# Graph network on one core: in the steps of passes 1 to 4, the gathered group ahead of the stored blocks on TensorE

## The reference

```python
edge_index = jnp.stack([src, dst])
x = _layernorm(x + _L0_gnn_ref(x, src, dst, edge_weight, ...), axis=-1)   # weighted sum over edges, two matrices
x = _layernorm(x + _L1_gnn_ref(x, edge_index, ...), axis=-1)              # three layers: sum, W1, relu, W2, layer norm
x = _layernorm(x + _L2_gnn_ref(x, ..., src, dst), axis=-1)                # sum with degrees, then top-2 of 64 experts, batch norm
x = _layernorm(x + _L3_gnn_ref(x, src, dst, edge_weight, ...), axis=-1)   # weighted sum over edges, one matrix
return x
```

## Time and profile before

| | |
|---|---|
| median of 3 runs | 5157.87 us |
| lowest, highest | 5154.81, 5174.32 us |
| span of the profiled execution | 5775.2 us |
| its own time | none given beside the span |
| TensorE, busy | 4680.6 us, 81% |
| VectorE, busy | 3836.1 us, 66% |
| GpSimd, busy | 3422.4 us, 59% |
| ScalarE, busy | 2434.9 us, 42% |

### The profile page before, as it was taken

How to read it: one execution, slowest core, us unless ns; L and a number is a source line. 1 busy time by engine, 2 the same in 40 slices (tenths; PEclk the granted TensorE clock), 3 DMA queues, 4 the chain that set the end, 5 groups by cost and what they waited for, 6 DMA issues and landing times. The chain is left out here.

```text
span 5775.2 us, 83539 instructions
## 1 busy us (share of the span) xinstructions
PE 4680.6 (81%) x25279; PEld 3860.8 (67%) x25279; DVE 3836.1 (66%) x12440; ACT 2434.9 (42%) x6047; POOL 3422.4 (59%) x3425
## 2 busy tenths in 40 slices
PE   4988986678888788877888788885799867999897
PEld 3777864478777566655666567664799735777775
DVE  6788888457777587746888635456789655444453
ACT  3888875333332233323444333331455413333332
POOL 5566666656665555666666566664345454666665
PEclk8999988889998899988999889997899968999998
DMA  5333333487778767787878877774668533333333
GB/s 149 109 113 118 113 121 118 149 254 222 222 225 282 216 201 208 213 273 244 247 242 243 296 240 220 224 219 144 223 214 264 165 81 104 98 98 98 96 98 88
DMA packets 545371, 1047.08 MB, mean 181 GB/s; under 512 B 105274, under 2 KB 308792, under 8 KB 544636
## 3 DMA queue, kind: packets, MB, share of 16 engines
q0 software_dynamic: 221664, 684.44, 40.7%
q1 hardware_dynamic: 305978, 341.48, 18.0%
q10 hardware_dynamic: 17280, 15.74, 0.8%
HBM read 927.95 MB, written 114.65 MB: 181 GB/s over the span
## 5 line engine op out<-in xcount | busy, mean ns | idle before, releaser
L2412 POOL DMA_INDIRECT slot_rows<-planes,REC x1800 | 1743.1, 968 | 1017.9 <-issue 476.5
L2964 ACT ACTIVATE wide_blocks<-HH 128x512 fp32r<-128x512 uint8 x1344 | 739.6, 573 | 1046.8 <-PE PS L2516 429.3
L2516 PE MATMUL PS<-plane_rows,wide_blocks 128*128 128x512 f32 x3528 | 1027.0, 432 | 172.2 <-ACT wide_blocks L2964 124.0
L2516 PEld LDWEIGHTS PS<-plane_rows,wide_blocks 128*128 128x128 f32 x3528 | 687.5, 203 | 368.0 <-ACT wide_blocks L2964 152.7
L2412 POOL DMA_INDIRECT ring<-in_x,REC x555 | 536.7, 967 | 313.0 <-issue 142.9
L2412 POOL DMA_INDIRECT ring<-table,REC x486 | 466.2, 959 | 320.2 <-issue 212.6
L2494 PE MATMUL PS<-ring,pick 128*128 128x256 f32 x2082 | 561.7, 405 | 64.3 <-DMA ring<-table,REC 25.5
L2581 PE MATMUL PS<-HH 128*128 128x256 f32 x2058 | 506.2, 388 | 7.8 <-issue 5.5
L2494 PEld LDWEIGHTS PS<-ring,pick 128*128 128x128 f32 x2082 | 404.6, 203 | 155.6 <-issue 51.7
L3122 DVE TENSOR_SCALAR slot_picks<-iotab,REC 128x128 fp32r<-128x128 bf16 x1800 | 413.1, 302 | 137.5 <-remote 71.1
L2929 ACT ACTIVATE HH<-iota,HH 128x128 bf16<-128x128 f32 (+1 forms) x962 | 329.2, 391 | 338.1 <-remote 176.4
(11 more groups left out here) (380 smaller groups left out, 8980.8 us busy)
## 6 DMA issues: line engine op xcount, KB each, us to landing
HH<-dense_blocks SPq DMA_DIRECT2D x672, 112.0 KB
HH<-in_L_gnn_w SPq DMA_DIRECT2D x128, 512.0 KB
plane_rows<-planes SPq DMA_DIRECT2D x64, 768.0 KB
planes<-HN SPq DMA_DIRECT2D x188, 256.0 KB
slot_rows<-planes,REC POOLq DMA_INDIRECT x1800
dense_blocks<-HH SPq DMA_DIRECT2D x24, 784.0 KB
expert_outputs<-ring ACTq DMA_DIRECT2D x120, 128.0 KB
ring<-in_x,REC POOLq DMA_INDIRECT x555
```

Source lines behind the costliest of these rows:

```text
L2412: pool.indirect_dma_start(to, None, planes[k] if dense else tables[k], bass.IndirectOffsetOnAxis(ap=at_rows, axis=0)).then_inc(s_slot[slot ...
L2516: last = mm(bank(5 + n % 2, RP), WIDE[:, at_block:at_block + P], plane(0, t, RP), start=t == 0, stop=t == NT - 1)
L2964: fn(WIDE[:, e % XA * XW:e % XA * XW + w], AB[n % QA][:, lo:lo + w], ACT.Copy).then_inc(s_ax, 1)
```

## The change

In each step of `one_pass` on TensorE, the call of `products` moves from behind the two calls of `dense` to ahead of them. In passes 0 and 5 there are no stored blocks in steps that have gathered groups, and the blocks of the extra steps at a pass's end have no group beside them, so these keep their order. No other engine's program changes.

```diff
             def one_pass(k):
                 for g in range(STEPS[k]):
+                    if g < GROUPS[k]:
+                        products(k, g)
                     if k in DENSE_PASSES:
                         dense(k, blocks(g))
                     if k < 4 and g >= GROUPS[k]:
                         dense(k + 1, head_blocks(g - GROUPS[k]))
-                    if g < GROUPS[k]:
-                        products(k, g)
                     if g == 1:
                         pe.wait_ge(s_w, w_count(k))
```

## The result

The changed kernel takes 5179.72 us (median) against 5158.84 us for the kernel before on the same chip: ratio 1.0035, 95% interval [1.0024, 1.0045]. That is 21 us slower by the medians and 18 us by the ratio, within the half per cent that was called no change, and 17.7 us above the forecast. One of its six executions took 15779 us; ratio and interval leave it out, and without it the median would be 5179.33 us.

The account below looks back on a forecast made before the run. TensorE was taken as busiest, idling before stored blocks. Terms 7.7 - 5.8 + 3 - 3 + 3 = +4.9 us of span, times 0.893 = +4.4, gave 5162 us; range 5118 to 5202.

Parts of the forecast that it names:

- What bounds the kernel now: TensorE busiest, 4680.6 of 5775.2 us; in the middles it idles before stored blocks, never before gathered groups.
- The order as a ring: Only the gathered group moves among stored blocks (D) and remaining work (E) on TensorE; whole-turn waits keep their length.
- Stored blocks waiting for ScalarE, -3 us: Middles: stored blocks sometimes gain 0.70 us where ScalarE was held by a copy or relu; ends nothing and 112 us.
- The start, +7.7 us: Four pass starts: step 0's stored blocks move behind the first gather's wait, 1.92 us each warm; 13.6 us in all cold.
- The tail, -5.8 us: Tails of passes 1 to 3: step 137's stored blocks, 1.92 us each, are hidden behind gathers; pass 4 gains nothing.
- SyncE and the DMA queues, +3 us: Pass ends: SyncE's plane reloads start 2.6 us later, taken as 1 us at each of three boundaries; worst 7.8.
- E nearer to D, +3 us: Layer and hidden groups follow stored blocks 0.70 us sooner and may wait for ScalarE, mainly pass 3; ends 0 and 206.
- VectorE's operand for a gathered tile, 0: Before the transposes: gathered group lies 1.92 us further ahead, but VectorE is busy, so no gain; ends -34.7 and 0.
- (a): Middles, faster: gathered groups fill waits before stored blocks, 80 to 112 us of span, about 5078 us; chance 0.14.
- (b): Middles, slower: layer and hidden groups wait for ScalarE, 0.70 us each, 59 us in all, 5211 us; chance 0.12.
- (c): Pass ends, slower: cold start, no tail gain, late reloads, 23 us, 5179 us; chance 0.06 beyond the bound.
- (d): TensorE, slower: a late gather holds stored blocks; 0.0 us in pass 4's trace, counted inside the forecast, no separate chance.

Follow-up runs that it names:

- the second profile: The kernel before, unchanged, run and profiled once more: 5159.29 us, ratio 0.9996.
- four pairs: Old against changed order: as they were, ScalarE's roots before widenings, four widened-piece places, both; changed order costs +0.35%, +0.25%, +0.19%, +0.14%.
- both edits: ScalarE's roots ahead of widenings plus four widened-piece places for three, against the kernel before: old order 5151.59 us (0.9978), changed order 5157.74 us (0.9992).

## Why the prediction was right or wrong

**The number held, the sum did not.** 5179.72 us lies in the range of 5118 to 5202 and inside the band of no change, which had 0.68. But the forecast was 5162, and none of its terms is where the 21 us came from: it was the width of the band that held, and not the sum.

**"What bounds the kernel now": half right.** TensorE is the busiest engine, but the idle time "before the stored blocks" came from a stretched execution. In an undisturbed one, idle before L2516 and L2519 is 14.8 and 7.2 us in all, and what TensorE waits for in the middles is VectorE: 36.3 us before the histogram (L2598 for L3310) in pass 2, 53.8 us before the transposes (L2619 for L3391) in pass 3. After the change these are 39.2 and 60.1 us. Nor is it so that "a gathered group never keeps anything waiting in the middle": in pass 1 of the second profile the gathered rows are what TensorE waits for most, 24.3 us. The 617 us were seen, and answered with a factor of 0.893 on the sum; a factor cannot mend which wait comes last. The text's caution, that part of the idle time need not exist in an undisturbed run, was right, and no term was changed for it.

**"The order as a ring": the step that failed.** It holds for TensorE, whose own turn stays the same. "Every wait that spans a whole turn keeps its length" does not hold for the other engines: ScalarE meets TensorE's ring at one point, the stored blocks, and VectorE at another, the layer product. The way from the layer product to what stands behind the widening grew by 0.70 us, as the example shows. The distance from E to D was priced, but only as something that TensorE could win (**"Stored blocks waiting for ScalarE, -3 us"**, ends 0 and -112). There was nothing to win, and what was queued behind the waiting widening on ScalarE, the root and the normalised rows, and VectorE behind these, was not listed. From the earlier trace rows the term read off that this wait is "a ring on itself"; it is, and it also holds whatever stands behind it in ScalarE's program.

**"The start, +7.7 us": 0.** The new order in step 0 alone gives 1.0000 [0.9991, 1.0009]. Stored blocks did move behind the wait, and slowly: nine in 3.84 us (step 0 has nine, not eight). The clock granted over these 3.84 us is 0.50, the lower of its two levels, and 1.00 in the blocks after the next group. From the changed kernel's timeline of TensorE at the start of pass 2:

```profile
1699.25 0.77 PE L2487 MATMUL PS<-slot_rows,slot_picks 128*128 128x512 f32 x1 [12.65 <-DMA slot_rows<-planes,REC]
1703.49 1.56 PE L2487 MATMUL PS<-slot_rows,slot_picks 128*128 128x512 f32 x2 [3.48 <-DMA slot_rows<-planes,REC]
1704.85 4.04 PE L2516 MATMUL PS<-plane_rows,wide_blocks 128*128 128x512 f32 x9
1708.69 1.41 PE L2487 MATMUL PS<-slot_rows,slot_picks 128*128 128x512 f32 x3
```

The wait for the first gather is 12.65 us with nothing in it, as the term had it. But the middle that follows does not end later for it: with this change alone the four middles are 0.7 to 3.3 us shorter than in the second profile of before, not 1.9 longer. The Trainium skill's rule weighed there (TensorE: Matmul & The Clock Gate, "HAM oscillation — how this bites in real kernels") is borne out in the slow blocks and not in the time: neither 7.7 nor 13.6 us arrived.

**"The tail, -5.8 us": 0.** Step 137 alone gives 1.0000 [0.9991, 1.0009], where 5.8 us would be 0.9989. Its stored blocks are not wholly hidden in the tail, which grows by 1.2 to 2.8 us with them in that kernel and by 0.4, -0.6 and 1.8 us in passes 1 to 3 of the changed one. Net with the start: 0, where +1.9 was summed. Pass 4 was right: "pass 4's grows by 2", measured 2.0 to 2.9 us in four pairs.

**"SyncE and the DMA queues, +3 us": not seen.** From the end of a pass's last group to the next pass's first it was 22.9, 24.7 and 34.4 us and is 23.9, 21.4 and 33.4: 3.3 us less in all.

**"E nearer to D, +3 us": not seen.** TensorE's wait at L2643 for the relu in the middle of pass 3 went from 16.0 to 13.7 us. ScalarE is ready for E; it is late behind D.

**"VectorE's operand for a gathered tile, 0": the sign was right**, no gain; the wait before L2619 grew by 6.3 us, as VectorE runs later.

**The rivals.** (a), faster: gone with the idle time on which it stood. (b), slower, E waits for ScalarE: not so, see L2643; but it was the only one to ask what stands behind a widening on ScalarE. It asked for TensorE's sake, and the one who waited was VectorE. (c), ends that do not cancel: its 5179 is what was measured, by accident, for the two ends alone each give 1.0000 and the reloads nothing. (d), a late gather holds stored blocks: 14.6 us more idle before L2487 in the whole kernel (85.1 to 99.7) and 12.4 less before L2516. In the middles it has not grown, as shown above; the two trade places outside them, and the long ones are the waits at the passes' starts.

**Of the signs named,** the slow blocks after step 0 and the tails of passes 1, 2 and 4 came out as said, and pass 3's tail grew by 1.8 us. That idle time before L2516 and L2519 "stays within 10% of 225 us" did not, and would not have in the unchanged kernel either. Nothing named would have shown the true cause, as no sign looked at VectorE's waits for ScalarE.

**What stays open.** With both edits about 6 us are left (0.14%, each ratio known to 0.1%). The tails of passes 3 and 4, which neither edit touches, are 2.5 and 2.1 us longer in the changed order of this pair (41.8 to 44.3, 46.8 to 48.8), as was expected of a part that does not pass through the widening; what in them costs it was not tried. Whether the rest is ScalarE's remaining waits (in the changed order the widening still waits 117.7 us in pass 3's middle, against 60.6 us) or nothing was not tried, nor were ScalarE's other events ahead of the widenings.

## What to carry to other kernels

When a step is moved on one engine, list for every other engine what it waits for from the moved work, and then what stands behind that wait in its own program: a producer that refills a ring (here the widening) passes its wait on to everything queued after it. Small work that another engine waits for, such as a root of 128 numbers, belongs ahead of such a refill; here that, or one more place in the ring, gave 0.2% in the unchanged order, and the two together no more. A profile that is 12% longer than the runs is to be taken anew before a wait is read from it.

## What was not expected of the hardware

The same kernel, profiled twice, had spans of 5775.2 and 5159.7 us. VectorE was busy as long (3836.1 and 3836.0 us), ScalarE nearly (2434.9 and 2480.1), and TensorE 166 us longer in the first (4680.6 and 4515.0). The rest lay in waits, and they fell on other pairs of engines: 65.4, 29.8, 45.3 and 85.0 us before the stored blocks in the first, 22.0 us there in the whole of the second. Waits that seem to name the bottleneck can be a property of one execution.

TensorE's busy time in a middle is not steady from profile to profile. In the changed kernel it is 5.2 us longer in pass 2 and 4.5 us longer in pass 3 than in the second profile of before, with the granted clock at 0.97 for 0.98 and 0.93 for 0.94, which looks like a second price of the order. But the two other kernels with the new order in these middles (all steps but 0, and passes 2 and 3 alone) have the clock at 0.98 and 0.94, as before, and are nearly as slow there (544.4 and 585.1, 542.3 and 586.3 us). So a price in the clock is not shown.
